# Reordered ScalarE, VectorE, TensorE and SyncE work in the feed-forward stage of a fused conditioning, attention and feed-forward kernel

## The reference

```python
x = x + attention(cond(x, itok_B_1_198))       # 16 heads, top-k keys per head
h = x @ W.T + adapter(x, itok_B_0_6)           # a low-rank adapter chosen per item
Wg, Wu, Wd = (lut[codes] * scales for each)    # 4-bit codes, one scale per 32 inputs
gate = h @ Wg.T                                # 512 -> 4096
up = h @ Wu.T                                  # 512 -> 4096
x = x + (gelu_tanh(gate) * up) @ Wd.T          # 4096 -> 512
```

## Time and profile before

| what | value |
| --- | --- |
| median of 3 runs | 2783.42 us (2781.2 to 2783.82) |
| the profiled execution | 2785.65 us |
| its span | 2784.1 us |
| granted TensorE clock, mean | 0.979 of full |
| TensorE busy (matmul) | 2606.1 us, 94% |
| VectorE / ScalarE / GpSimd busy | 1922.3 / 891.4 / 1002.4 us |

### The profile page before, as it was taken

How to read it: one execution, slowest core, us unless ns; L and a number is a source line. 1 busy time by engine, 2 the same in 40 slices (tenths; PEclk the granted TensorE clock), 3 DMA queues, 4 the chain that set the end, 5 groups by cost and what they waited for, 6 DMA issues and landing times.

```text
span 2784.1 us, 38774 instructions
## 1 busy us (share of the span) xinstructions
PE 2606.1 (94%) x13824; PEld 2175.8 (78%) x13824; DVE 1922.3 (69%) x3084; ACT 891.4 (32%) x1530; POOL 1002.4 (36%) x1189
## 2 busy tenths in 40 slices
PE   5898989899889999999899999998999999999998
PEld 4787878788667777788778778777888888888887
DVE  6877787777567777887777788777754545445454
ACT  3444545455322222222222222222222222222222
POOL 3454444534345544655554465545410000000000
PEclk8999999999999999999999999999999999999999
DMA  3223222222788888668787966678555644574363
GB/s 117 90 88 101 89 99 88 96 95 87 262 297 307 332 329 319 246 234 309 263 311 290 331 252 227 224 257 318 192 195 204 261 178 157 210 275 153 146 251 130
DMA packets 173618, 585.34 MB, mean 210 GB/s; under 512 B 22137, under 2 KB 81401, under 8 KB 139009
## 3 DMA queue, kind: packets, MB, share of 16 engines
q1 hardware_dynamic: 138112, 481.17, 47.6%
q0 software_dynamic: 35328, 101.82, 9.9%
HBM read 446.14 MB, written 136.71 MB: 209 GB/s over the span
## 4 chain that ended last, share of the span: by engine, by line
PE 46%; issue 23%; POOL 15%; DVE 7%; DMA 6%; ACT 1%; POOLq 1%; SPq 0%; DVEq 0%; ACTq 0%
PE proj L693 12%; PE down L883 11%; PE bank_a L866 11%; DMA w_scratch<-w_parts 6%; POOL w_parts L559 5%; PE bank_b L866 5%; PE bank_c L866 3%; POOL w_parts L557 3%; POOL lut_v L567 2%; POOL scales L529 1%; PE scores L733 1%; PE pv L758 1%; PE scores L742 1%; POOL lut_v L574 1%; POOL packed L527 1%
## 5 line engine op out<-in xcount | busy, mean ns | idle before, releaser
L883 PE MATMUL down<-d_slot,inter_parts 128*128 128x512 f32 x3072 | 771.0, 394 | 2.2 <-issue 2.2
L883 PEld LDWEIGHTS down<-d_slot,inter_parts 128*128 128x128 f32 x3072 | 583.7, 191 | 129.8 <-issue 7.6
L1404 DVE TENSOR_TENSOR acc<-down,acc 128x512 f32<-128x512 f32 x512 | 352.4, 688 | 344.6 <-PE down L883 324.2
L866 PE MATMUL bank_a<-h_ahead,gu_slot 128*128 128x512 f32 x1536 | 406.3, 401 | 68.0 <-ACT copy_p L1092 55.5
L1092 ACT ACTIVATE copy_p<-bank_a 128x512 f32<-128x512 f32 x384 | 228.1, 594 | 655.4 <-PE bank_a L866 655.3
L866 PEld LDWEIGHTS bank_a<-h_ahead,gu_slot 128*128 128x128 f32 x1536 | 293.0, 193 | 140.6 <-ACT copy_p L1092 66.4
L866 PE MATMUL bank_a<-h_once,gu_slot 128*128 128x512 f32 x1536 | 390.1, 389 | 1.4 <-ACT copy_p L1092 1.4
L866 PEld LDWEIGHTS bank_a<-h_once,gu_slot 128*128 128x128 f32 x1536 | 288.1, 188 | 62.2 <-ACT copy_p L1092 2.5
L574 POOL TENSOR_TENSOR lut_v<-lut_v,signed_scale 128x512 f32<-128x512 f32 x96 | 124.6, 1298 | 499.7 <-DVE lut_v L1185 499.0
L1389 DVE TENSOR_TENSOR up<-gate,up 128x512 f32<-128x512 f32 x256 | 237.4, 927 | 72.3 <-ACT gate L1102 58.9
L1109 ACT ACTIVATE inter_parts<-up 128x512 fp32r<-128x512 f32 x256 | 161.6, 631 | 361.8 <-DVE up L1389 224.3
(11 more groups left out here) (123 smaller groups left out, 3446.2 us busy)
## 6 DMA issues: line engine op xcount, KB each, us to landing
gu_slot<-w_scratch SPq DMA_DIRECT2D x128, 1792.0 KB, 8.3
d_slot<-d_scratch SPq DMA_DIRECT2D x64, 1024.0 KB, 11.2
w_scratch<-w_parts POOLq DMA_DIRECT2D x96, 512.0 KB, 5.1
h_ahead<-h_scratch SPq DMA_DIRECT2D x44, 1024.0 KB, 11.9
h_once<-h_scratch SPq DMA_DIRECT2D x33, 1024.0 KB, 5.0
h_scratch<-h_out SPq DMA_DIRECT2D x32, 896.0 KB, 5.0
acc<-out SPq DMA_DIRECT2D x22, 1024.0 KB, 5.4
out<-acc SPq DMA_DIRECT2D x22, 1024.0 KB, 12.3
```

What stands on the lines that cost most here:

```text
L866: ins = pe.matmul(bank[:], gu_slot[n % 2][:, w, u, c * P:(c + 1) * P], mat(v, h)[:, c, part, :], start=(start and c == 0 and i == 0), stop ...
L883: ins = pe.matmul(bank[:], inter_parts[:, j, u, q, e * P:(e + 1) * P], d_slot[m % 2][:, j, part, :], start=(j == 0 and i == 0), stop=(j == ...
L1404: dve.tensor_tensor(acc[:, q, e], down[turn % 4][:], acc[:, q, e], ALU.add).then_inc(acc_added, 1)
```

## The change

Five things, all in the feed-forward stage. ScalarE does the three copies before the GELUs, and the high parts of a unit at the end of that unit instead of in the next. TensorE has all four down chunks in the second half of the unit, around p3. VectorE does operation 7 of a weight unit in the next unit, right behind `gate_first`, and the product of SECOND_HALF and its low part in the unit itself. `acc` takes the place in SBUF that `h_ahead1` had, and SyncE loads the first `acc` ahead of the last two stores of h. ScalarE's wait for the last stored x goes.

```diff
             h_once = sb("h_once", [P, NM - AHEAD_MATS, 2, 2, HALF], F32R)
-            h_ahead.append(sb("h_ahead1", [P, AHEAD_MATS, 2, 2, HALF], F32R))
+            acc = sb("acc", [P, 2, NE, D], F32)
...
-            acc = sb("acc", [P, 2, NE, D], F32)
+            h_ahead.append(sb("h_ahead1", [P, AHEAD_MATS, 2, 2, HALF], F32R))
...
             load_down(0)
+            for q in (SECOND_HALF, FIRST_HALF):
+                load_acc(0, q)
             store_hidden(NT - 1, 0)
             store_hidden(NT - 1, 1)
             for q in h_stored:
                 sp.wait_ge(q, NT * 16)
             sp.wait_ge(x1_stored, NT * 16 + PRIMED)
-            for q in (SECOND_HALF, FIRST_HALF):
-                load_acc(0, q)
...
                 product(n, a, W_S2, H_T2, start=False).then_inc(p6_full, 1)
-                down_of_last_block(0)
                 if n >= 1:
                     pe.wait_ge(up_added[FIRST_HALF], n)
                 product(n, bank_b, W_S3, H_T3).then_inc(p7_full, 1)
-                down_of_last_block(1)
                 pe.wait_ge(p6_copied, n + 1)
                 product(n, a, W_S1, H_T1, start=False).then_inc(p5_full, 1)
+                down_of_last_block(0)
+                down_of_last_block(1)
+                pe.wait_ge(p5_copied, n + 1)
+                product(n, a, W_S4, H_B22, start=False).then_inc(p3_full, 1)
                 down_of_last_block(2)
                 down_of_last_block(3)
-                pe.wait_ge(p5_copied, n + 1)
-                product(n, a, W_S4, H_B22, start=False).then_inc(p3_full, 1)
...
-            act.wait_ge(x1_stored, NT * 16 + PRIMED)
             for n in range(NU):
-                if n >= 1:
-                    inter_high(n - 1, SECOND_HALF)
                 copy_product(n, p1_full, copy_p1, p1_copied, gate_added[FIRST_HALF])
-                if n >= 1 and n % 2 == 0:
-                    inter_high(n - 1, FIRST_HALF)
-                gelu_first(n)
                 copy_product(n, p6_full, copy_p6, p6_copied, up_added[FIRST_HALF])
                 if n == 0:
                     hidden_high(NT - 1, 0)
+                elif n % 2 == 0:
+                    inter_high(n - 1, FIRST_HALF)
                 copy_product(n, p5_full, copy_p5, p5_copied, up_added[SECOND_HALF])
+                gelu_first(n)
+                gelu_second(n)
                 if n == 0:
                     hidden_high(NT - 1, 1)
+                inter_high(n, SECOND_HALF)
                 if n % 2 == 1:
                     inter_high(n - 1, FIRST_HALF)
-                gelu_second(n)
-            inter_high(NU - 1, SECOND_HALF)
...
+            def dequantised(n, first, last):
+                if 0 <= n < len(LATE):
+                    dequantise(*LATE[n], first, last)
...
                 if n >= 1:
-                    gelu_times_up(n - 1, SECOND_HALF)
                     up_first(n - 1)
                     gelu_times_up(n - 1, FIRST_HALF)
-                    inter_low(n - 1, SECOND_HALF)
                 gate_first(n)
+                if n == 0:
+                    hidden_low(NT - 1, 0)
+                dequantised(n - 1, DQ - 1, DQ)
+                dequantised(n, 0, 2)
                 if n >= 1 and j == 0:
                     inter_low(n - 1, FIRST_HALF)
-                if n == 0:
-                    hidden_low(NT - 1, 0)
-                dequantised(0, 2)
+                dequantised(n, 2, 4)
+                up_second(n)
                 add_down(m - 1, NE * j)
-                dequantised(2, 5)
+                dequantised(n, 4, 6)
                 add_down(m - 1, NE * j + 1)
-                dequantised(5, 6)
-                up_second(n)
+                dequantised(n, 6, 7)
+                gelu_times_up(n, SECOND_HALF)
                 if n == 0:
                     hidden_low(NT - 1, 1)
-                dequantised(6, 7)
                 add_down(m - 1, NE * j + 2)
-                dequantised(7, DQ)
-                add_down(m - 1, NE * j + 3)
-                if j == 1:
+                if j == 0:
+                    add_down(m - 1, NE * j + 3)
+                    inter_low(n, SECOND_HALF)
+                else:
+                    inter_low(n, SECOND_HALF)
+                    add_down(m - 1, NE * j + 3)
                     inter_low(n - 1, FIRST_HALF)
```

More of the change, by code:

```diff
@@ L1406, in _ @@
             LATE = [(c, k) for c in range(EARLY, NCP) for k in range(6)]
+            def dequantised(n, first, last):
+                if 0 <= n < len(LATE):
+                    dequantise(*LATE[n], first, last)
             for n in range(NU):
                 m, j = divmod(n, 2)
-                def dequantised(first, last):
-                    if n < len(LATE):
-                        dequantise(*LATE[n], first, last)
                 if n >= 1:
-                    gelu_times_up(n - 1, SECOND_HALF)
                     up_first(n - 1)
                     gelu_times_up(n - 1, FIRST_HALF)
-                    inter_low(n - 1, SECOND_HALF)
                 gate_first(n)
+                if n == 0:
+                    hidden_low(NT - 1, 0)
+                dequantised(n - 1, DQ - 1, DQ)
+                dequantised(n, 0, 2)
                 if n >= 1 and j == 0:
                     inter_low(n - 1, FIRST_HALF)
-                if n == 0:
-                    hidden_low(NT - 1, 0)
-                dequantised(0, 2)
+                dequantised(n, 2, 4)
+                up_second(n)
                 add_down(m - 1, NE * j)
-                dequantised(2, 5)
+                dequantised(n, 4, 6)
                 add_down(m - 1, NE * j + 1)
-                dequantised(5, 6)
-                up_second(n)
+                dequantised(n, 6, 7)
+                gelu_times_up(n, SECOND_HALF)
                 if n == 0:
                     hidden_low(NT - 1, 1)
-                dequantised(6, 7)
                 add_down(m - 1, NE * j + 2)
-                dequantised(7, DQ)
-                add_down(m - 1, NE * j + 3)
-                if j == 1:
+                if j == 0:
[4 more added lines that the diff above has]
+                    add_down(m - 1, NE * j + 3)
                     inter_low(n - 1, FIRST_HALF)
-            gelu_times_up(NU - 1, SECOND_HALF)
             up_first(NU - 1)
             gelu_times_up(NU - 1, FIRST_HALF)
-            inter_low(NU - 1, SECOND_HALF)
             inter_low(NU - 1, FIRST_HALF)
```

## The result

| | median of the runs | lowest to highest | ratio to before, 95% interval |
| --- | --- | --- | --- |
| before | 2783.18 us | 2781.2 to 2783.82 | |
| changed kernel | 2748.39 us | 2745.64 to 2750.14 | 0.9869 (0.9855 to 0.9883) |

The change gains 34.8 us, inside the predicted range (2692 to 2764), but it is only half of the 67 us between the median before and the forecast of 2716. The profiled execution of the changed kernel took 2745.64 us with a span of 2744.1 us, and the granted clock is 0.984 where it was 0.979; over the four runs of the changed kernel it is 0.979 to 0.984, so that the mean clock alone tells little.

What follows compares the result with a forecast made beforehand. TensorE's own work was the floor, 110.5 us of the stage above it. 86 (stall) - 8 - 18 (late loads) + 6 (start) + 2.2 (end) = 68 us off 2785.65 gave 2717.6, written as 2716; range 2692 to 2764.

Steps and rivals of the forecast that it cites:

- The stall and its cause: VectorE's lut_v waits for GpSimd, delaying product, high part, copy and TensorE: 53.4 us waits, 33 us lower clock, 86 us.
- What stays of the stall, 8 us: Stall cost left on TensorE's path after the change, between bounds of none and 30 us, taken as 8 us.
- the lower bound: None of the stall stays: GpSimd's waits for stores go, a stall is near 1.2 us and stays hidden.
- Hidden wait of 3.7 us: Wait at lut_v that TensorE would not feel with the new VectorE order: 3.7 us where it was 1.3.
- What is late next, 18 us: At changes of visit the FIRST_HALF acc store holds up SyncE, so gu_slot lands late: 18 us over seven turns.
- the bound of 34 us: Upper bound for late gu_slot loads at changes of visit: seven turns of 4.9 us each.
- 2 us for a turn: TensorE's wait for late gu_slot taken for each of seven turns, with 4 us of lower clock in all.
- Start 6 us, end 2.2 us: Gains from loading acc earlier at the stage's start (5.4 to 7.4, taken 6) and losing the 2.23 us wait at its end.
- VectorE as the bound: Rival: waits inside VectorE's unit make it the bound, slower than before, about 2800 us at 16.5 us a unit; chance 0.07.
- The stores stay slow: Rival: store waits and late gu_slot loads stay at upper bounds, gain 30 us, 2754; chance 0.25 shared with little room.
- Everything is hidden: Rival: no stall and no late load on TensorE, gain 96 us, 2688; chance 0.14.
- It doesn't do what it says: Rival: p6 still waits for a high part behind VectorE, hidden wait 2, 2765; chance 0.25 shared with slow stores.

Runs made afterwards that it cites:

- e6: Changed kernel with the four loads of h matrices ahead in units 3, 4, 4, 5 of a visit instead of 1 to 4; 2697.5 us.
- e1: Changed kernel with SyncE's wait for the FIRST_HALF store and the load of acc moved behind the next unit's gu_slot load; 2745.7 us.
- e12: Changed kernel with the four h loads ahead in units 2, 3, 4, 5 of a visit, so only unit 1's leaves the turn; 2721.57 us.
- e13: Changed kernel with the four h loads ahead in units 1, 3, 4, 5 of a visit, so only unit 2's leaves the turn; 2718.73 us.
- e4: Changed kernel with operation 7 back in its own weight unit, behind the third add; 2731.19 us.
- e8: e4 with the four h loads ahead in units 3, 4, 4, 5 of a visit instead of 1 to 4; 2731.46 us.
- e9: Kernel before with only the four h loads ahead moved to units 3, 4, 4, 5 of a visit; 2788.6 us.

## Why the prediction was right in sign and too high in size

- *The stall and its cause: right.* 53.4 us of waits and 33 us of lower clock were to go. With quiet turns 91.1 us go, start (5.1) and end (2.2) included, so 83.8 are left for the stall, by subtraction.
- *What stays of the stall, 8 us: the lower bound was true.* The three waits for copies that are left (4.2 us) all lie in units 0 and 1. It came by the way of the lower bound more than by hiding: the wait stayed in number (24) but fell from 3.4 us in the mean to 0.7, where the bound had 1.2, since the chains with three splits hardly wait for stores any more (1.9 us in all). But the sign "GpSimd's wait for stores well below 55 us" failed: 48.9 us in 26 stay, and 59.3 in e6. They only moved, to weight units behind which GpSimd has time, as at 941.00. The sign of a clock above 0.98 up to the last weight failed too; it is 0.98.
- *Hidden wait of 3.7 us: consistent.* In e6 `lut_v` waits up to 4.0 us, and behind units 0 and 1 TensorE waits for no copy and no `up`. In the changed kernel itself, where the longest is 1.4, it was hardly needed.
- *What is late next, 18 us: this is the step that failed.* Place and sign were right, the size was 50.7 us: the stage takes 1985.0 us in the changed kernel and 1934.3 in e6 (lines below). The nine waits for `gu_slot` behind unit 2 are 43.4 - 4.75 = 38.7 us, against 2.5 in e6, and the units behind six of them take 14 us more than at the higher clock level. I had 14 us of waits and 4 of clock. The seven turns wait 6.20, 5.37, 6.17, 0.98, 5.88, 7.13 and 3.93 us, 5.1 in the mean. The 4.9 us worked out from the earlier trace rows were near that, and so the bound of 34 us was near the 35.7 us that the turns wait; but partly by luck, since the turn worked out is the one that waits 0.98 us, and the bound had no lower clock in it.

```profile
757.47 1.62 PE L867 MATMUL bank_a<-h_ahead,gu_slot 128*128 128x512 f32 x6 [0.52 <-issue]
...
2680.77 11.04 PE L884 MATMUL down<-d_slot,inter_parts 128*128 128x512 f32 x48
```

- *Why 2 us for a turn was wrong.* I took it since "the median store lands before the next unit starts", 13.2 us. Those rows mix two kinds of store. In the first turn of before, SyncE goes on 9.8 us after the store of SECOND_HALF is issued, and 14.8 after that of FIRST_HALF, the one in question:

```profile
875.47 0.40 SPq L429 DMA_DIRECT2D out<-acc  x1
885.23 0.38 SPq L426 DMA_DIRECT2D acc<-out  x1
...
890.78 0.40 SPq L429 DMA_DIRECT2D out<-acc  x1
905.62 0.38 SPq L426 DMA_DIRECT2D acc<-out  x1
```

  The five of each kind in the earlier trace rows take 9.0 to 12.4 and 14.0 to 19.1 us; the median lies between the kinds, and in none of the seven turns of before did the store of FIRST_HALF land before the next unit started. Counted from the first unit of the visit, the late `gu_slot` lands at 65.7 us before and at 65.6 in the changed kernel (means of seven turns); what moved is TensorE, due at 65.8 before and at 60.5 now. So the stalls had covered nearly all of the lateness at every turn. I also took the lateness for a matter of SyncE's list, in which a store that lands early frees it; the queues were at their rate, and e1, e6, e12 and e13 show that the amount decides.
- *Start 6 us, end 2.2 us: right.* 5.1 and 2.2. Unit 2 starts at 784.49, 0.7 us later than the later of my two times.
- *The sum.* 68 + 5.8 (stall) - 32.7 (late loads) - 0.9 (start) = 40.2, against 40.4 in the stages of the profiled executions. This only books the difference: stall and late loads are both measured against e6, so it would close whatever their causes.
- *VectorE as the bound: no.* It is busy 968.01 us over 4927 / 66 = 74.7 units, 13.0 us a unit, and TensorE waits for no `up`. Its product fell to 928 ns in the mean from 1083: before, 28 of the 145 products ran while GpSimd scaled `lut_v` and took 1.71 us in the mean, now none of the 150 does.

```profile
L1386 DVE TENSOR_TENSOR up<-gate,up 128x512 f32<-128x512 f32 x150 | 139.1, 928 | 16.5 <-ACT gate L1102 8.2
```

- *"The stores stay slow", 2754, is nearest to the time, and for half of its reason:* the late loads alone, without the stalls. "Everything is hidden", 2688, is near what the change does once h is loaded later (2697.5). "It doesn't do what it says", 2765, is out, since copies cost nothing behind unit 1.

What stays open is which part of the traffic costs the rate in the turn, GpSimd's stores or the two holes of SyncE, and how much of the stall's end is the shorter wait and how much the new order behind it: no run separates them.

## What to carry to other kernels

When a stall goes, ask which queue used it to catch up: price what comes next by bytes per unit of the busiest stretch and by the very transfer that is waited for, not by a median over transfers of different places. If moving a late load forward only makes another one late, the amount is the limit, and loads with slack should leave that stretch. A part of a change that looks harmful alone (operation 7, 17 us against e4) may be the best part once the next limit is moved (34 us against e8).

## What the runs showed that I had not expected

The place of one VectorE operation decides in which weight units GpSimd waits for its stores: in those with three splits wherever operation 7 stands in its own unit (before, e4, e8, e9), mostly in others where it stands in the next (the rest; the highest share in those with three splits is 11.0 of 59.3 us, in e6). The totals are alike, 54.3 to 61.3 us in the first group and 43.0 to 59.4 in the second. And a wait of 6.20 us cost more than its length: the 12 matmuls behind it show 2.93 and 1.79 us, where the first six behind a wait of 1.00 us show 1.67.
